# Two scans of 512 elements joined into one of 1024, in two states of three, in a Mamba block followed by a gated feed-forward network

## The reference

```python
def step(h, inp):
    xt, dt_t, B_t, C_t = inp
    A_disc = jnp.exp(A[None, None, :] * dt_t[:, :, None])
    h = A_disc * h + dt_t[:, :, None] * B_t[:, None, :] * xt[:, :, None]
    y_t = jnp.einsum('bed,bd->be', h, C_t) + D * xt
    return (h, y_t)
```

## Time and profile before

| what | value |
|---|---|
| median of three runs | 2822.73 us (2822.26 to 2822.75) |
| the profiled execution's own time | 2821.17 us |
| its span, first instruction to last | 2819.5 us |
| busy share of the span | PE 93%, DVE 83%, ACT 69%, POOL 65% |
| instructions of line 1165 | 1024 |
| mean granted clock of TensorE | 0.983 |

### The profile page before, as it was taken

How to read it: one execution, slowest core, us unless ns; L and a number is a source line. 1 busy time by engine, 2 the same in 40 slices (tenths; PEclk the granted TensorE clock), 3 DMA queues, 4 the chain that set the end, 5 groups by cost and what they waited for, 6 DMA issues and landing times.

```text
span 2819.5 us, 49137 instructions
## 1 busy us (share of the span) xinstructions
PE 2623.1 (93%) x17154; PEld 2337.7 (83%) x17154; DVE 2349.9 (83%) x3053; ACT 1944.3 (69%) x4040; POOL 1840.3 (65%) x1546
## 2 busy tenths in 40 slices
PE   6678999999999999999999999999978999999998
PEld 4557888888888888888888888888868888888887
DVE  4899999999999999999999999999985455555554
ACT  6888888888888888888888888888866322222221
POOL 3788888888888888888888888888874000000000
PEclk8789999999999999999999999999989999999999
DMA  6111122121221221112112121121132322222211
GB/s 227 42 42 46 57 63 67 57 70 60 61 68 58 64 62 58 58 60 70 57 62 68 57 72 58 61 65 58 54 128 68 114 81 90 83 83 90 90 61 31
DMA packets 130154, 198.78 MB, mean 71 GB/s; under 512 B 16368, under 2 KB 93296, under 8 KB 129904
## 3 DMA queue, kind: packets, MB, share of 16 engines
q1 hardware_dynamic: 129904, 195.57, 21.9%
HBM read 144.68 MB, written 50.86 MB: 69 GB/s over the span
## 4 chain that ended last, share of the span: by engine, by line
PE 49%; ACT 21%; DVE 15%; issue 9%; DMA 1%; POOL 0%; DVEq 0%; ACTq 0%; SPq 0%; POOLq 0%
PE banks L1479 17%; PE banks L1441 9%; DVE h L1165 8%; PE banks L1453 6%; DVE acc L1178 5%; ACT banks L1028 5%; PE banks L1491 4%; PE banks L1357 4%; PE banks L1341 4%; PE banks L1379 2%; ACT act_high L990 2%; PE banks L1427 2%; ACT g L927 1%; ACT L865 1%; ACT L876 1%
## 5 line engine op out<-in xcount | busy, mean ns | idle before, releaser
L1165 DVE TENSOR_TENSOR_SCAN h<-banks,ub 128x512 f32<-128x512 f32 x1024 | 1203.2, 1209 | 75.5 <-ACT banks L1028 61.3
L768 POOL TENSOR_TENSOR ub<-u,b_row 128x1020 f32<-128x1020 f32 x512 | 1215.4, 2374 | 0.1
L1028 ACT ACTIVATE banks<-dt,neg_a 128x510 f32<-128x510 f32 x1024 | 695.0, 684 | 59.0 <-DVE h L1165 59.0
L1178 DVE SCALAR_TENSOR_TENSOR acc<-banks,c_tok,acc 128x512 f32<-128x512 f32 x1024 | 712.6, 738 | 9.6 <-issue 5.1
L1453 PE MATMUL banks<-ident,h 128*128 128x128 f32 x4096 | 580.5, 276 | 71.8 <-DVE acc L1178 69.6
L1453 PEld LDWEIGHTS banks<-ident,h 128*128 128x128 f32 x4096 | 478.4, 143 | 119.4 <-DVE h L1165 68.0
L1441 PE MATMUL banks<-act_high,h_rounded 128*128 128x256 f32 x2048 | 525.0, 294 | 13.3 <-ACT z_out L805 9.0
L1441 PE MATMUL banks<-act_low,h_rounded 128*128 128x256 f32 x2048 | 499.3, 282 | 0.0
L1441 PEld LDWEIGHTS banks<-act_high,h_rounded 128*128 128x128 f32 x2048 | 389.7, 190 | 14.2 <-ACT z_out L805 9.3
L1479 PE MATMUL banks<-act_high,h_rounded 128*128 128x512 f32 x1024 | 398.9, 390 | 0.0
L1479 PE MATMUL banks<-act_low,h_rounded 128*128 128x512 f32 x1024 | 398.9, 390 | 0.0
(11 more groups left out here) (126 smaller groups left out, 4287.6 us busy)
## 6 DMA issues: line engine op xcount, KB each, us to landing
b_row<-b_scratch SPq DMA_DIRECT2D x128, 512.0 KB, 4.3
z_scratch<-z_out SPq DMA_DIRECT2D x128, 256.0 KB, 3.5
zl<-z_scratch SPq DMA_DIRECT2D x32, 1024.0 KB, 8.0
x_sb<-in_x SPq DMA_DIRECT2D x32, 256.0 KB, 3.1
x_res<-in_x SPq DMA_DIRECT2D x32, 256.0 KB, 4.9
h_full<-in_h SPq DMA_DIRECT2D x2, 4096.0 KB, 16.5
x_scratch<-x_sb SPq DMA_DIRECT2D x32, 256.0 KB, 2.2
xr<-x_scratch SPq DMA_DIRECT2D x16, 512.0 KB, 4.8
```

The source lines that it names most:

```text
L768: nc.gpsimd.tensor_tensor(ub[:, n % 2, :, 1:], u[:, :, 1:], b_row[:, n // QUARTER % 2, n % QUARTER:n % QUARTER + 1, 1:].to_broadcast([P, E ...
L1028: nc.scalar.activation(decay_half(k)[:, :, 1:], dt[:, par, 2 * i:2 * i + 2, 1:], ACT.Exp, scale=neg_a[:, n:n + 1]).then_inc(decay_ready, 1)
L1165: nc.vector.tensor_tensor_scan(h[:, n % 2, 2 * i:2 * i + 2].rearrange("p e t -> p (e t)"), banks[:, k % DECAYS, :], ub[:, n % 2, 2 * i:2 * ...
L1178: nc.vector.scalar_tensor_tensor(out=acc[:, par, q], in0=turned[q], scalar=c_tok[:, par, q, n:n + 1], in1=acc[:, par, q], op0=ALU.mult, op ...
```

## The change

For two of three states both halves of the decay lie in neighbouring banks (0 and 1, or 1 and 2), and one scan of 1024 columns takes the place of two of 512. The third state (banks 2 and 0) keeps its two scans. With s = 16c + n, a state keeps two scans when s mod 3 is 1, that is when (c + n) mod 3 is 1. The joined scan waits for both halves of the decay, counts `scan_done` up by two at its end, and the pieces that stood between the two scans are called behind it.

```diff
+        def scans(n):
+
+            k = 2 * n
+            return [(k, 2)] if k % DECAYS + 1 < DECAYS else [(k, 1), (k + 1, 1)]
...
-                    for i in range(2):
-                        k = 2 * (NS * c + n) + i
-                        dve.wait_ge(decay_ready, k + 1)
-                        nc.vector.tensor_tensor_scan(h[:, n % 2, 2 * i:2 * i + 2].rearrange("p e t -> p (e t)"), banks[:, k % DECAYS, :],
-                                                     ub[:, n % 2, 2 * i:2 * i + 2].rearrange("p e t -> p (e t)"), 0.0, ALU.mult, ALU.add).then_inc(scan_done, 1)
+                    for k, pieces in scans(NS * c + n):
+                        i = k % 2
+                        dve.wait_ge(decay_ready, k + pieces)
+                        nc.vector.tensor_tensor_scan(h[:, n % 2, 2 * i:2 * (i + pieces)].rearrange("p e t -> p (e t)"),
+                                                     banks[:, k % DECAYS:k % DECAYS + pieces, :].rearrange("p b f -> p (b f)"),
+                                                     ub[:, n % 2, 2 * i:2 * (i + pieces)].rearrange("p e t -> p (e t)"), 0.0, ALU.mult, ALU.add).then_inc(scan_done, pieces)
                         if n >= 1:
-                            between(3 * (n - 1) + i)
+                            for m in range(i, i + pieces):
+                                between(3 * (n - 1) + m)
```

## The result

The changed kernel takes 2973.75 us (2972.07 to 2980.6, 4 runs) against 2822.74 before, a ratio of 1.0538 (95% interval 1.0523 to 1.0553): 151 us slower. The forecast was 2913 us, with a range of 2843 to 2965. The direction was right, the loss came out 1.7 times as large as the sum, and the time lies above the range.

The account below looks back on a forecast made before the run. It took a chain bound by DVE, with PE close, then by ACT between states 8 and 13. Stalls of 116.3 us less 25.6 gained gave 90.7 us more, a forecast of 2913 us, range 2843 to 2965.

Parts of the forecast that it names:

- What bounds the kernel: DVE is full from state 13 to state 8 of the next chunk; from state 8 to 13 ACT sets the pace.
- state 11: In ACT's stretch, the joined scan holds back the second decay half of state 12: 22 × 0.5 = 11.0 us.
- State 8: Joined scan waits for its late second decay half; `gated`, and `act_high` behind it, 2.8 us later: 22 × 2.8 = 61.6 us.
- State 13: DVE already waits for the second half; the whole joined scan comes after it, 1.0 us later: 21 × 1.0 = 21.0 us.
- States 5 and 7: State 5 holds back state 6's second decay half, 22 × 0.6 = 13.2 us; state 7 costs 5.0 us where 8 is split.
- State 7 joined with 8 split: The joined scan waits for its second decay half, only in chunks where state 8 keeps two scans: 10 × 0.5 = 5.0 us.
- The other states: The 1.39 us of `add_y` covers the wait for a decay half, costing nothing as long as ACT is free.
- states 0 and 1: Both joined: state 1's second decay half comes late with no `add_y` between the scans to hide it, 10 × 0.45 = 4.5 us.
- The join: A joined scan takes 2.21 us against 2.33 for two, saving 0.12; 213 joins in DVE's stretch gain 25.6 us.
- The clock: Rival: PE's clock falls after its wait at state 8, 1.2 us a chunk, 40 us in all: 2953 us; 8 in 100.
- DVE's work alone decides: Rival: shifts are absorbed and only the joins' saving on DVE stays, 2782 to 2797 us, faster; 8 in 100.
- The stall stays on DVE: Rival: at state 8 ACT loses only DVE's own 1.8 us, held-back halves cost nothing: 35 us, 2858 us; 22 in 100.

## Why the prediction was right in kind and wrong in size

**What bounds the kernel.** Right. Taking the chain to be on DVE up to state 8 and on ACT from there to 13 priced state 11 as a loss although DVE has time there, and the run with 11 alone confirmed it (14.5 us, forecast 11.0).

**State 8.** Right in each step of the chain: DVE's wait is 1.93 us (forecast 1.8), the wait of `act_high` grows by 2.98 (2.8), a chunk at full clock by 3.0. 22 × 0.2 = 4 us too little.

**State 13.** 1.11 and 1.14 us a chunk, forecast 1.0: 21 × 0.12 = 3 us too little.

**States 5 and 7.** 5 alone costs 0.51 (forecast 0.6) and 7 with 8 split 0.63 (0.5). Wrong was the step "*State 7 joined with 8 split* (10 chunks)", which left state 7 out where 5 is joined too. There it costs 1.1 us on top (1.62 less 0.51), 11 × 1.1 = 12 us. In the changed kernel, where 8 is late as well, state 9 starts 4.02 us late with c mod 3 = 1 and 3.20 with c mod 3 = 0, so 0.8 of it is left: 9 us.

**The other states.** "In the other states the 1.39 us of `add_y` covers the wait for a decay half" failed at state 15 too, joined in 21 chunks: DVE waits 0.35 to 0.39 us there for the second half (0 before), and some 0.2 of it is still there at the end of the chunk, about 5 us. No run had states 0 and 1 alone (forecast 0.45 in 10 chunks). In the trace of the change, state 2 starts 0.27 us late with c mod 3 = 2, and 0.11 to 0.17 early in the other chunks, which fits.

**The join.** "So I take 0.12" failed: it is 0.05, which the estimate by the rule of the Trainium skill named in the prediction gives (half throughput of the scan, "DVE: opcode table, instruction layouts, handler registers and perf-mode slots", Datapath and trigger behaviour), and the trace agrees with 2.28 us. What the joins gave in the end is the difference to the kernel with the same waits, release and order and two scans: 12 to 14 us in all, 0.32 and 0.35 us in the chunks at full clock (4.24 against 4.56, 2.48 against 2.83), which makes about 10. Of the 25.6 us of gain 12 to 15 were missing.

**The clock.** The largest step that is missing from the sum. It stood as a rival with 8 in 100, spread as 2% over all of PE's work. What happens is local, 16 falls. One of 3.4 us costs 1.1: 7.06 against 5.99 in chunk 4, the one full chunk with c mod 3 = 1 behind the start of the pipeline, and 5.2 to 5.3 against 4.24 with c mod 3 = 0. The two of 6.8 us cost 2.1 and 2.6. That is 14 × 1.1 + 4.7 = 20 us. The rival had PE's wait at state 8 as its cause, and that is where 15 of the 16 come; but giving it as an alternative to the forecast, and not as a term of it, was the error, since the falls come with the stalls that the forecast itself counts on.

**The sum again.** With 4 (state 8), 3 (13), 4 (11), 9 to 12 (7), 5 (15), 12 to 15 (the join) and 20 (the clock) the sum of 90.7 becomes 148 to 154, where 151 were measured. The terms are rounded, and two chunks at the start lose less than the later ones of their kind, so that an error of some us either way could hide in it. By this account the steps that took the time out of its range are the clock, which was no term, the saving of a join at 0.12, and state 7 at nothing behind a joined 5.

**The rivals.** "DVE's work alone decides" fell with the result, which is slower. "The stall stays on DVE" fell with the wait of 3.22 us on ACT and with the 3.0 us, not 1.8, that a chunk loses with state 8 alone joined.

**What was said to be seen.** 341 and 342 scans came out, the long ones at 2.28 us; DVE is busy for 89 to 91% of the steady part (forecast 92); the chunk's losses, forecast as 3.1, 4.1 and 1.2 by c mod 3, are 4.2 to 5.7, 7.06 and 2.48, in the same order.

## What to carry to other kernels

Joining two instructions saves their fixed cost once and makes three other things coarser: the start waits for the later input, the buffer comes free at the later end, and the work between them moves behind. Each cost more here than the 0.05 us that a join saves (95, 57 and 57 us over 341 joins): before a join, read for each place when the second input is there against the first instruction's start, and who waits for the first one's end. And where TensorE works nearly without a gap, as here (286.5 of 300 us), a new wait on another engine that stops it is to be counted with the clock that it may cost, as a term of the sum.

## What the runs showed of the hardware

A scan of 1024 float32 columns whose decay spans two banks of PSUM took 2284 ns, against 1206 to 1209 for 512 within one bank: 1.08 us for 512 more columns, so the second bank shows no cost of its own. With a loss of 3 us in a chunk of 65 (state 8 joined) TensorE's granted clock dropped to half for some 3.4 us in part of the chunks, and with losses of 0.5 to 1.6 us it did too (states 5 and 7 joined, 7 falls), while 1.1 us at state 13 went with one fall in the whole run. What PE did before: it stood 3.10 us in the first case and 1.96 in the second, each in one piece. What decides between a chunk with a fall and one without, with the same wait of 3.10 us on PE, these runs do not tell.
